# Four-layer graph network on one core: the edge stage's second bias goes through the TensorE accumulator, and VectorE forms a message in one instruction

## The chip, the cores and the metric

The kernel runs on one core of one Trainium2 chip. The metric is the device time of one execution in microseconds (us), lower is better. Where a profile is read, it is one execution on the same core; its time stands beside the median of the timed runs, so that the two are not mixed.

## The reference, cut to what matters

Four graph layers follow each other on 3125 nodes and 103125 edges, sorted by their destination. The change touches only the third, in which every edge builds a message from its source node and its own 64 attributes, and the messages are summed at the destination:

```
ei   = concat(x[src], edge_attr)                  # one row of 256 + 64 per edge
core = maximum(ei @ W1 + b1, 0.0) @ W2 + b2        # b2: the second layer's bias
gate = sigmoid(ei @ Wg + bg)
msg  = gate * core
agg  = segment_sum(msg, dst)
out  = agg + x, then a layer norm with gamma and beta
```

All of it is float32. `b2` is one row of 256 numbers, the same for each edge.

## The kernel before, in words

Each layer is one or more stages, and a stage ends with all engines meeting. The stage of the change is `edge_mlp_pass` (L1539). The node part of `ei @ [W1, Wg]` with its biases has been computed for each node ahead of it and lies in DRAM as `p_table`, 512 numbers a row. The pass then walks over the edges in 102 supertiles of 1024, each of 8 tiles of 128 edges. A loop over 51 pairs of supertiles is unrolled by two, and within a supertile the work is written out in four steps, `k` = 0 to 3, of two tiles each, `y` = 0 and 1. The order on each engine is as written; nothing is rescheduled.

In a step the engines do this for the tile `y`, and PE, DVE and ACT are two tiles (one step) apart from stage to stage:

- PE multiplies the transposed edge attributes (64 rows) by the weights into `psP` (L1756): tile 0 from partitions 0 to 63, tile 1 from partitions 64 to 127.
- DVE adds the gathered node row and writes `pre` (L1659). `pre` holds 256 numbers for the hidden layer and 256 for the gate.
- ACT takes the sigmoid of the second half into `gate` (L1713).
- PE transposes the first half into `psR` (L1770), ACT applies the relu while it copies that into `rT` (L1718), and PE multiplies it by `W2` into `psC` (L1762): two products per tile, each a float32 product of 128 rows by 256 columns.
- DVE adds `b2`, which lies in SBUF copied to all 128 partitions, to `psC` and writes `whole` (L1667), then multiplies `whole` by `gate` in place (L1669). `Link` (L59) makes the second wait for the first.
- ACT rounds two tiles of `whole` to float32r, the high part of `msg` (L1722); POOL subtracts to get the low part (L1595).

Once in a supertile, in step 0, PE transposes the next supertile's attributes (`psEA`, L1731) and DVE builds the one-hot matrix `hot` of the supertile before (L1674 and the helper L763). In step 2 PE sums that supertile's messages with `hot` into `psM`, 16 float32r products (L1737). Where a supertile's destinations span more than one block of 128 nodes, which happens 24 times, there is a round after step 3: DVE adds `psM` to the node sums (L1457), shifts the indices (L1684), builds `xhot`, PE sums again.

The waits that matter: PE's `psP` products wait for DVE's `pre` of the step before (L1753), its `W2` products for `rT` and for the message of the tile that last used the same `psC` (L1759, L1760), its sums for POOL's low parts (L1780). SyncE loads weights and the bias once (L1620 to L1623) and edge attributes per supertile.

Of the kernel before, what the change touches and what calls it, by code (L numbers as in the profile page):

```python
# [19 lines left out]
F32 = mybir.dt.float32  # L20
F32R = mybir.dt.float32r
BF16 = mybir.dt.bfloat16
I32 = mybir.dt.int32
ALU = mybir.AluOpType
# [3 lines left out]
P = 128  # L28
D = 256
# [21 lines left out]
START = 16  # L51
# [23 lines left out]
def hold(eng, sem):  # L75

    eng.sem_inc(sem, 1)


def gnn(nc, a, out, n_nodes, n_edges):  # L80
# [638 lines left out]
    held = top.enter_context(nc.semaphore("held"))  # L719
# [75 lines left out]
    def typed_pass():  # L795

        HALF = SLOTS // 2
        G = H0 * RELS
# [3 lines left out]
        with Stage(("idx_staged", "hotrow", "expanded", "x_hotrow", "x_expanded", "expand_read", "rows_read", "scored",  # L802
# [19 lines left out]
            pick = st.sb("pick", [T_LANES, WT])  # L822
            att = st.sb("att", [P, UT, 2, HALF, H0])
            et = st.sb("et", [P, HALF, 2, UT, G])
# [714 lines left out]
    def edge_mlp_pass():  # L1539
# [1 line left out]


        with Stage(("onehot", "x_onehot", "pre_ps", "pre", "gate", "rT_ps", "rT", "core", "msg", "summed", "added", "x_summed",
                    "x_added", "idx_staged", "high", "split", "link_dve", "link_act", "zeroed", "eaT_ps", "eaT"), ("w_in", "ea0", "ea1")) as st:
            S = st.sem
            DEEP = 4
            LATE = 2
            G_DEEP = SLOTS
            HALF = SLOTS // 2
            table_tile = st.sb("table_tile", [P, 1])  # L1550
            rows = st.sb("rows", [P, 2 * SLOTS, 2 * D])
            stage_idx = st.sb("stage_idx", [P, 2, SLOTS], I32)
# [4 lines left out]
            eaT = st.sb("eaT", [P, 2, HALF, P])  # L1557
            wb = st.sb("wb", [P, 2 * D])
            w2 = st.sb("w2", [P, 2, D])
            b2 = st.sb("b2", [P, D])  # L1560
            pre = st.sb("pre", [P, DEEP, 2 * D])
            gate = st.sb("gate", [P, G_DEEP, D])
            rT = st.sb("rT", [P, DEEP, 2, P])
            whole = st.sb("whole", [P, DEEP, D])
# [4 lines left out]
            psC = [st.ps(f"psC{n}", [P, 512]) for n in range(2)]  # L1569
# [5 lines left out]
            with nc.Block() as block:  # L1575
# [41 lines left out]
                @block.sync  # L1617
                def _(sp):
                    for lo in (0, DE):
                        sp.dma_start(wb[lo:lo + DE, 0:D], a["l2_w1"][D:D + DE, :]).then_inc(S["w_in"], 16)  # L1620
                        sp.dma_start(wb[lo:lo + DE, D:2 * D], a["l2_wg"][D:D + DE, :]).then_inc(S["w_in"], 16)
                    sp.dma_start(w2[:, :, :], a["l2_w2"].rearrange("(c p) d -> p c d", p=P)).then_inc(S["w_in"], 16)
                    sp.dma_start(b2[:, :], a["l2_b2"].partition_broadcast(P)).then_inc(S["w_in"], 16)  # L1623
                    view = a["ea"].rearrange("(s p j) d -> p s (j d)", p=P, j=SLOTS)
                    sp.dma_start(ea[:, 0, :], view[:, 0, :]).then_inc(S["ea0"], 16)
                    with sp.Fori(0, PAIRS) as i:
                        for u in range(2):
                            s = 2 * i + u
                            sp.wait_ge(S["eaT_ps"], START + s)
                            sp.dma_start(ea[:, 1 - u, :], view[:, ds(s + 1, 1), :].squeeze(1)).then_inc(S[f"ea{1 - u}"], 16)  # L1630
                    sp.wait_ge(S["ea0"], 16 * PAIRS + 16)

                @block.vector
                def _(dve):
                    v = nc.vector
                    link = Link(dve, S["link_dve"])

                    v.memset(msg[:, :, :, :, :].bitcast(F32), 0.0)
                    v.memset(hot[:, :, :].bitcast(F32), 0.0)
                    for tile in (table_tile, pre, gate, rT, whole, NODE, psC[0], psC[1]):  # L1640
                        last = v.memset(tile[:, :, :, :] if len(tile.shape) == 4 else
                                        tile[:, :, :] if len(tile.shape) == 3 else tile[:, :], 0.0)
                    last.then_inc(S["zeroed"], 1)
                    dve.wait_ge(S["zeroed"], START + 1)
                    dve.wait_ge(S["w_in"], 96)
                    with dve.Fori(0, PAIRS) as i:
                        for u in range(2):
                            s = 2 * i + u
                            x0, x1, b0, more = work_of(dve, s)
                            link.turn()  # L1650
                            for k in range(HALF):
                                t = SLOTS * s + 2 * k
                                for y in range(2):
                                    j = 2 * k + y
                                    rows_in(dve, i, u, [j])
                                    dve.wait_ge(S["pre_ps"], START + t + y + 1)
                                    dve.wait_ge(S["rT_ps"], START + t + y - DEEP + LATE + 1)
                                    dve.wait_ge(S["gate"], START + t + y - DEEP + 1)
                                    v.tensor_tensor(pre[:, j % DEEP, :], psP[y][:, :], rows[:, u * SLOTS + j, :],  # L1659
                                                    ALU.add).then_inc(S["pre"], 1)  # L1660
                                if k == LATE:
                                    dve.wait_ge(S["summed"], START + s)
                                for y in range(2):
                                    q = (2 * k + y - 2 * LATE) % SLOTS
                                    dve.wait_ge(S["core"], START + t + y + 1)
                                    dve.wait_ge(S["split"], START + HALF * s + k - 1)
                                    link(v.tensor_tensor(whole[:, q % DEEP, :], psC[y][:, 0:D], b2[:, :], ALU.add))  # L1667
                                    dve.wait_ge(S["gate"], START + t + y - 2 * LATE + 1)
                                    v.tensor_tensor(whole[:, q % DEEP, :], whole[:, q % DEEP, :], gate[:, q % G_DEEP, :],  # L1669
                                                    ALU.mult).then_inc(S["msg"], 1)  # L1670
                                if k == 0:
                                    dve.wait_ge(S["summed"], START + s)
                                    hold(dve, held)
                                    link(v.tensor_copy(rel[:, :], dst_of(s - 1)))  # L1674
                                    one_hot(hot[:, :, :], rel[:, :]).then_inc(S["onehot"], 1)
                                if k == HALF - 1:
                                    dve.wait_ge(S["summed"], START + s + 1)
                                    add_block(b0, psM[:, 0:D]).then_inc(S["added"], 1)
                                    dve.wait_ge(S["added"], START + s + 1)
                                    hold(dve, held)  # L1680
                                    with dve.If(more):
                                        with dve.Fori(x0, x1) as x:
                                            link.turn()
                                            link(v.tensor_scalar(rel[:, :], rel[:, :], -float(P), None, ALU.add))  # L1684
                                            one_hot(xhot[:, :, :], rel[:, :]).then_inc(S["x_onehot"], 1)
                                            dve.wait_ge(S["x_summed"], START + x + 1)
                                            add_block(b0 + 1 + x - x0, psM[:, 0:D]).then_inc(S["x_added"], 1)
                                            dve.wait_ge(S["x_added"], START + x + 1)
                                    link.turn()
# [38 lines left out]
                def _(pe):  # L1728
# [9 lines left out]
                                                        start=(j == 0 and n == 0), stop=(j == SLOTS - 1 and n == 1))  # L1738
                        return last

                    pe.wait_ge(S["w_in"], 96)
                    pe.wait_ge(S["zeroed"], START + 1)
                    pe.wait_ge(S["ea0"], 16)
                    transpose_ea(0)
                    with pe.Fori(0, PAIRS) as i:
                        for u in range(2):
                            s = 2 * i + u
                            x0, x1, _, more = work_of(pe, s)
                            for k in range(HALF):
# [4 lines left out]
                                for y in range(2):  # L1754
                                    lo = y * DE
                                    nc.tensor.matmul(psP[y][:, :], eaT[lo:lo + DE, u, k, :], wb[lo:lo + DE, :], start=True,  # L1756
                                                     stop=True).then_inc(S["pre_ps"], 1)
                                for y in range(2):
                                    pe.wait_ge(S["rT"], START + t + y - 1)  # L1759
                                    pe.wait_ge(S["msg"], START + t + y - 1)  # L1760
                                    for c in range(2):
                                        last = nc.tensor.matmul(psC[y][:, 0:D], rT[:, (2 * k + y) % DEEP, c, :], w2[:, c, :],  # L1762
                                                                start=(c == 0), stop=(c == 1))
                                    last.then_inc(S["core"], 1)

                                for y in range(2):
# [978 lines left out]
```

## Time and profile before

| what | value |
|---|---|
| median of 3 runs | 10081.02 us (10074.35 to 10107.51) |
| the profiled execution, its own time | 10087.5 us |
| its span, first to last instruction | 10085.6 us |
| mean granted TensorE clock in it | 0.763 |
| loop of the changed stage | 4026 to 5988 us of the span |

The page gives busy time for each engine. A row of a group gives place, engine, operation and tiles, the shape, the count, the busy time and the mean of one, and behind the last bar how long the engine had been idle before such instructions and who ended that. PE is the matrix product, PEld the load of its stationary operand; one float32 product shows as two records of each (two passes), a float32r product as one. In a row of the timeline the first number is the start, the second the length of the whole run of records.

### The profile page before, as it was taken

The page shows a single profiled execution, that of the slowest core. Times are in us where ns is not written, and L with a number is a line of the kernel's source. Part 1 is how long each engine was busy: PE and PEld are TensorE (multiplying, and loading weights), DVE is VectorE, ACT ScalarE, POOL GpSimd, SP SyncE. Part 2 cuts the span into 40 slices and gives each one's busy share as a digit, 9 for nine tenths or more (in the row PEclk, how much of TensorE's full clock was granted, in tenths as well). Part 3 has the DMA queues.
Part 4 walks back from the last instruction along what each step waited for, and adds up shares of the span by engine and source line. Part 5 has one row for each costly group of instructions (what it writes and reads, how often), then busy time and mean ns, then how long its engine had stood idle before and what let it go on. Part 6 is the DMA issues. An engine that isn't in the chain of part 4 may idle for free. (4 is left out here: it accounts for less than half of the span.)

```text
span 10085.6 us, 117611 instructions
## 1 busy us (share of the span) xinstructions
PE 6095.2 (60%) x25212; PEld 4519.3 (45%) x25213; DVE 5155.4 (51%) x9537; ACT 2745.0 (27%) x6077; POOL 4589.4 (46%) x4782
## 2 busy tenths in 40 slices
PE   4867777753444455989898863454554445455544
PEld 2445656541333343666666642343443333343433
DVE  3258888733222223777777764444344544344444
ACT  0134444421000002444444442222122122222221
POOL 0046555501665640767777742444443233444432
PEclk9978888875776766999999985666666666666666
DMA  3367777711222321444444422332332232332322
GB/s 114 115 193 222 223 217 219 201 47 34 84 85 83 88 69 46 127 119 123 123 122 122 124 82 80 93 93 86 95 93 84 62 92 87 91 92 85 96 83 70
DMA packets 440369, 1100.23 MB, mean 109 GB/s; under 512 B 102512, under 2 KB 177365, under 8 KB 439479
## 3 DMA queue, kind: packets, MB, share of 16 engines
q0 software_dynamic: 249344, 763.23, 26.8%
q1 hardware_dynamic: 190636, 333.56, 10.1%
q14 instruction: 358, 2.93, 0.1%
q8 instruction: 31, 0.51, 0.0%
HBM read 1014.51 MB, written 81.94 MB: 109 GB/s over the span
## 5 line engine op out<-in xcount | busy, mean ns | idle before, releaser
L779 POOL DMA_INDIRECT st_rows<-g_table,st_stage_idx x1632 | 1550.8, 950 | 2019.3 <-DVE st_msg L2385 1541.6
L2564 PE MATMUL st_psM<-st_msg,st_hot 128*128 128x273 f32 x3264 | 1004.1, 470 | 402.6 <-DVE node_values L2338 182.3
L886 POOL DMA_INDIRECT st_rows<-kv_table,st_stage_idx x832 | 825.4, 992 | 590.9 <-PE st_psM L1254 275.5
L2564 PEld LDWEIGHTS st_psM<-st_msg,st_hot 128*128 128x128 f32 x3264 | 747.8, 233 | 629.1 <-issue 413.1
L1586 POOL DMA_INDIRECT st_rows<-p_table,st_stage_idx x816 | 801.6, 982 | 261.4 <-issue 163.5
L779 POOL DMA_INDIRECT st_rows<-h_table,st_stage_idx x816 | 777.9, 953 | 263.2 <-issue 260.8
L1762 PE MATMUL st_psC<-st_w,st_rT 128*128 128x256 f32 x3264 | 815.4, 393 | 0.5 <-DVE st_whole L1669 0.5
L1762 PEld LDWEIGHTS st_psC<-st_w,st_rT 128*128 128x128 f32 x3264 | 587.8, 190 | 381.9 <-ACT st_rT L1718 203.8
L1659 DVE TENSOR_TENSOR st_pre<-st_psP,st_rows 128x512 f32<-128x512 f32 x816 | 524.5, 685 | 409.5 <-PE st_psP L1756 280.2
L1595 POOL TENSOR_TENSOR st_msg<-st_whole,st_msg 128x512 fp32r<-128x512 f32 x408 | 565.0, 1385 | 350.4 <-ACT st_msg L1722 343.3
L2477 ACT ACTIVATE st_low<-st_dm 128x8 f32<-128x8 f32 x252 | 51.9, 206 | 2459.4 <-DVE st_dm L2328 1982.6
L1522 PE MATMUL st_psM<-st_rows,st_hot 128*128 128x256 f32 x1632 | 443.2, 434 | 365.5 <-issue 123.6
L1228 PE MATMUL st_psE<-st_q_rows,st_hotrow 104*128 104x256 f32 x1664 | 548.6, 502 | 42.2 <-issue 33.6
L2396 DVE TENSOR_TENSOR_SCAN st_psX<-st_pens,st_psX 24x1024 f32<-24x1024 bf16 x68 | 155.2, 2283 | 790.8 <-DMA h_table<-st_h 388.2
L1522 PEld LDWEIGHTS st_psM<-st_rows,st_hot 128*128 128x128 f32 x1632 | 358.0, 222 | 448.0 <-issue 325.1
L1713 ACT ACTIVATE st_gate<-st_pre 128x256 f32<-128x256 f32 x816 | 330.0, 416 | 761.7 <-DVE st_pre L1659 742.3
L1756 PE MATMUL st_psP<-st_wb,st_eaT 64*128 64x512 f32 x1632 | 472.2, 656 | 56.4 <-DVE st_pre L1659 50.2
L1228 PEld LDWEIGHTS st_psE<-st_q_rows,st_hotrow 104*128 104x128 f32 x1664 | 424.0, 261 | 145.4 <-issue 53.1
L2594 PE MATMUL st_psW<-ident,st_seg 24*128 24x24 f32 x544 | 61.7, 257 | 701.5 <-DVE st_seg L2397 701.5
L2385 DVE TENSOR_TENSOR st_msg<-st_rows,st_psU 128x2048 f32<-128x2048 f32 x204 | 464.8, 2279 | 2.0 <-ACT st_psU L2503 2.0
L2564 PE MATMUL st_psZ<-st_msg,st_xhot 128*128 128x273 f32 x768 | 309.6, 558 | 217.5 <-issue 137.2
L1254 PE MATMUL st_psM<-st_rows,st_hot 128*128 128x262 f32 x1632 | 397.7, 398 | 66.7 <-issue 56.0
(406 smaller groups left out, 11630.1 us busy)
## 6 DMA issues: line engine op xcount, KB each, us to landing
st_dst_row<-in_dst_row SPq DMA_DIRECT2D x310, 512.0 KB
kv_table<-st_rows_out SPq DMA_DIRECT2D x25, 1560.0 KB, 5.6
st_ea<-in_ea SPq DMA_DIRECT2D x103, 256.0 KB
st_rows<-g_table,st_stage_idx POOLq DMA_INDIRECT x1632
st_pens<-pen_table SPq DMA_DIRECT2D x208, 72.0 KB
st_rows<-kv_table,st_stage_idx POOLq DMA_INDIRECT x832
st_rows<-h_table,st_stage_idx POOLq DMA_INDIRECT x816
st_rows<-p_table,st_stage_idx POOLq DMA_INDIRECT x816, 3.5
```

What stands on the lines that cost most here:

```text
L779: pool.indirect_dma_start(out=rows[:, slot, j, :], out_offset=None, in_=table, in_offset=bass.IndirectOffsetOnAxis(ap=stage_idx[:, g, u * ...
L886: pool.indirect_dma_start(out=rows[:, slot, j, :], out_offset=None, in_=kv_table, in_offset=bass.IndirectOffsetOnAxis(ap=stage_idx[:, g, u ...
L1228: last = nc.tensor.matmul(psE[h][:, j * D:(j + 1) * D], onehots[0:NQ, h * HALF + j, :], queries, start=(fresh and j % 2 == 0), stop=True, ...
L1254: last = nc.tensor.matmul(out[:, 0:SUM_W], onehots[:, j, :], rows[:, slot, j, D:D + SUM_W], start=(j == 0), stop=(j == SLOTS - 1))
L1522: last = nc.tensor.matmul(out[:, 0:D], onehots[:, j, :], rows[:, slot, j, :], start=(j == 0), stop=(j == SLOTS - 1))
L1586: pool.indirect_dma_start(out=rows[:, u * SLOTS + j, :], out_offset=None, in_=p_table, in_offset=bass.IndirectOffsetOnAxis(ap=stage_idx[:, ...
L1595: nc.gpsimd.tensor_tensor(msg[:, half, q:q + 2, 1, :], whole[:, q % DEEP:q % DEEP + 2, :], msg[:, half, q:q + 2, 0, :].bitcast(F32), ALU.s ...
L1659: v.tensor_tensor(pre[:, j % DEEP, :], psP[y][:, :], rows[:, u * SLOTS + j, :], ALU.add).then_inc(S["pre"], 1)
L1756: nc.tensor.matmul(psP[y][:, :], eaT[lo:lo + DE, u, k, :], wb[lo:lo + DE, :], start=True, stop=True).then_inc(S["pre_ps"], 1)
L1762: last = nc.tensor.matmul(psC[y][:, 0:D], rT[:, (2 * k + y) % DEEP, c, :], w2[:, c, :], start=(c == 0), stop=(c == 1))
L2385: v.tensor_tensor(msg[:, u, :, 0:GAT_W].rearrange("p j (h c) -> p j h c", h=H3)[:, :, :, 0:HW3 - 1], rows[:, slot, :, 0:D].rearrange("p j ...
L2564: last = nc.tensor.matmul(out[:, 0:MSG_W], onehots[:, j, :], msg[:, u, j, :], start=(j == 0), stop=(j == SLOTS - 1))
```

## The change

The bias is no longer added by DVE. SyncE loads it twice, into partitions 0 and 32 of a tile `b2_in` of 33 rows that DVE has cleared. DVE makes `b2` from it in float32r: row 0 is the rounded value (the high half), row 32 the remainder (the low half), the rest are zeros. For each tile of edges PE first multiplies a block of ones (33 by 128) by `b2` (33 by 256) into `psC`, as the start of the accumulation, and the two `W2` products add to it. DVE then reads `psC` and `gate` and writes the finished message to `whole` in one instruction.

```
-            b2 = st.sb("b2", [P, D])
+            b2_in = st.sb("b2_in", [B_ROWS, D])          # B_ROWS = LOW + 1 = 33
+            b2 = st.sb("b2", [B_ROWS, D], F32R)
+            ones_b = st.sb("ones_b", [B_ROWS, P], F32R)
...
-                    sp.dma_start(b2[:, :], a["l2_b2"].partition_broadcast(P)).then_inc(S["w_in"], 16)
+                    sp.wait_ge(S["cleared"], START + 1)
+                    for row in (0, LOW):
+                        sp.dma_start(b2_in[row:row + 1, :], a["l2_b2"].unsqueeze(0)).then_inc(S["w_in"], 16)
...
+                    v.memset(ones_b[:, :].bitcast(F32), 1.0)
+                    v.memset(b2_in[:, :], 0.0).then_inc(S["cleared"], 1)
...
+                    link(v.tensor_copy(b2[:, :], b2_in[:, :]))
+                    v.tensor_tensor(b2[LOW:B_ROWS, :], b2_in[LOW:B_ROWS, :], b2[LOW:B_ROWS, :].bitcast(F32),
+                                    ALU.subtract).then_inc(S["bias"], 1)
...
-                                    link(v.tensor_tensor(whole[:, q % DEEP, :], psC[y][:, 0:D], b2[:, :], ALU.add))
+                                    hold(dve, held)
                                     dve.wait_ge(S["gate"], START + t + y - 2 * LATE + 1)
-                                    v.tensor_tensor(whole[:, q % DEEP, :], whole[:, q % DEEP, :], gate[:, q % G_DEEP, :],
+                                    v.tensor_tensor(whole[:, q % DEEP, :], psC[y][:, 0:D], gate[:, q % G_DEEP, :],
                                                     ALU.mult).then_inc(S["msg"], 1)
...
+                    pe.wait_ge(S["bias"], START + 1)
...
                                     pe.wait_ge(S["rT"], START + t + y - 1)
                                     pe.wait_ge(S["msg"], START + t + y - 1)
+                                    nc.tensor.matmul(psC[y][:, 0:D], ones_b[:, :], b2[:, :], start=True, stop=False)
                                     for c in range(2):
                                         last = nc.tensor.matmul(psC[y][:, 0:D], rT[:, (2 * k + y) % DEEP, c, :], w2[:, c, :],
-                                                                start=(c == 0), stop=(c == 1))
+                                                                start=False, stop=(c == 1))
```

On PE the change shows in each step of the loop. This is step 0 of a supertile before, from the top of the loop's body; `psC` are the `W2` products, `psP` and `psEA` those of the attributes.

```order
L1756 MATMUL st_psP<-st_wb,st_eaT 128x512 x2
L1759 REGISTER_ALU
L1762 MATMUL st_psC<-st_w,st_rT 128x256 x4
L1770 MATMUL st_psR<-ident,st_pre 128x128 x4
L1774 ISA
L1731 MATMUL st_psEA<-ident,st_ea 128x128 x4
```

And the same place now, where the line numbers have moved by 12 or 13:

```order
L1768 MATMUL st_psP<-st_wb,st_eaT 128x512 x2
L1771 REGISTER_ALU
L1773 MATMUL st_psC<-st_b,st_ones_b 128x256
L1775 MATMUL st_psC<-st_w,st_rT 128x256 x2
L1773 MATMUL st_psC<-st_b,st_ones_b 128x256
L1775 MATMUL st_psC<-st_w,st_rT 128x256 x2
L1783 MATMUL st_psR<-ident,st_pre 128x128 x4
L1787 ISA
L1742 MATMUL st_psEA<-ident,st_ea 128x128 x4
```

One short product stands behind `psP` and another between the two tiles' `W2` products; nothing else has moved on PE.

On DVE, in step 0 between `pre` and the next step's `pre`, this stands before; `rel` and `hot` are the indices and the one-hot matrix:

```order
L1659 TENSOR_TENSOR st_pre<-st_psP,st_rows 128x512
L1666 REGISTER_ALU
L1667 TENSOR_TENSOR st_whole<-st_psC,st_b 128x256
L1669 TENSOR_TENSOR st_whole<-st_whole,st_gate 128x256
L1667 TENSOR_TENSOR st_whole<-st_psC,st_b 128x256
L1669 TENSOR_TENSOR st_whole<-st_whole,st_gate 128x256
L1672 REGISTER_ALU
L1674 ISA
L1674 COPY st_rel<-dst_rel 128x8
L763 TENSOR_TENSOR st_hot<-st_rel,iota_row 128x1024
```

And now:

```order
L1670 TENSOR_TENSOR st_pre<-st_psP,st_rows 128x512
L1677 REGISTER_ALU
L1680 TENSOR_TENSOR st_whole<-st_psC,st_gate 128x256 x2
L1683 REGISTER_ALU
L1685 ISA
L1685 COPY st_rel<-dst_rel 128x8
L763 TENSOR_TENSOR st_hot<-st_rel,iota_row 128x1024
```

Four instructions on `whole` have become two; their place among the others is the same.

## Rows read from the trace of the kernel before

**Rows 1.** The page: busy time of the engines, and the granted TensorE clock by slices.
```profile
PE 6095.2 (60%) x25212; PEld 4519.3 (45%) x25213; DVE 5155.4 (51%) x9537; ACT 2745.0 (27%) x6077; POOL 4589.4 (46%) x4782
...
PEclk9978888875776766999999985666666666666666
```

**Rows 2.** The loop's stretch: length, busy PE, PEld, DVE, ACT, POOL, clock, DMA.
```profile
4026.00:5988.00 1962.00, 1764.19 (x8950) 1239.97 (x8948) 1416.28 (x2826) 942.50 (x2241) 1369.16 (x1313) 0.97 0.42 121
```

**Rows 3.** Groups of that stretch: count, busy us, mean ns, idle us before.
```profile
L1762 PE MATMUL st_psC<-st_w,st_rT 128*128 128x256 f32 x3264 | 815.4, 393 | 0.5 <-DVE st_whole L1669 0.5
...
L1595 POOL TENSOR_TENSOR st_msg<-st_whole,st_msg 128x512 fp32r<-128x512 f32 x407 | 563.8, 1385 | 346.4 <-ACT st_msg L1722 339.3 <-issue 2.3
...
L1669 DVE TENSOR_TENSOR st_whole<-st_whole,st_gate 128x256 f32<-128x256 f32 x816 | 391.4, 480 | 27.9
L1667 DVE TENSOR_TENSOR st_whole<-st_psC,st_b 128x256 f32<-128x256 f32 x816 | 339.0, 415 | 1.2 <-PE st_psC L1762 1.2
...
L1722 ACT CAST st_msg<-st_whole 128x512 fp32r<-128x512 f32 x407 | 252.1, 619 | 206.4 <-DVE st_whole L1669 171.9 <-issue 23.7
...
L1737 PEld LDWEIGHTS st_psM<-st_msg,st_hot 128*128 128x128 f32 x1632 | 201.0, 190 | 66.7 <-issue 66.6
...
L1737 PE MATMUL st_psM<-st_msg,st_xhot 128*128 128x256 f32 x384 | 83.3, 400 | 97.4 <-DVE st_xhot L763 97.4
...
L1731 PEld LDWEIGHTS st_psEA<-ident,st_ea 128*128 128x128 f32 x408 | 47.7, 142 | 0.0
```

**Rows 4.** Waits of that stretch: us in total, times, longest.
```profile
PEld st_psP L1756 <- DVE st_pre L1659: 86.9, 135, 1.1
```

**Rows 5.** Timeline of PE over one supertile: start, length of the run.
```profile
5008.87 0.60 PE L1770 MATMUL st_psR<-ident,st_pre 128*128 128x128 f32 x4
5009.30 0.60 PE L1731 MATMUL st_psEA<-ident,st_ea 128*128 128x128 f32 x4
5009.83 1.13 PE L1756 MATMUL st_psP<-st_wb,st_eaT 64*128 64x512 f32 x4
5010.89 1.99 PE L1762 MATMUL st_psC<-st_w,st_rT 128*128 128x256 f32 x8
5012.72 0.60 PE L1770 MATMUL st_psR<-ident,st_pre 128*128 128x128 f32 x4
5013.47 1.13 PE L1756 MATMUL st_psP<-st_wb,st_eaT 64*128 64x512 f32 x4
...
5017.35 2.17 PE L1737 MATMUL st_psM<-st_msg,st_hot 128*128 128x256 f32 x16 [0.40 <-POOL st_msg L1595]
5019.46 1.13 PE L1756 MATMUL st_psP<-st_wb,st_eaT 64*128 64x512 f32 x4
```

**Rows 6.** Timeline of PEld where the attribute product waits for nobody.
```profile
5022.87 0.30 PEld L1756 LDWEIGHTS st_psP<-st_wb,st_eaT 64*128 64x128 f32 x4 [0.17 <-issue]
```

**Rows 7.** PE in an early stage: a 35-row float32r product between 128-row ones.
```profile
380.73 2.54 PE L661 MATMUL st_psY<-st_w,st_hT 128*128 128x256 f32 x11
383.20 0.38 PE L664 MATMUL st_psY<-st_b,st_hot 35*128 35x256 f32 x1
383.51 0.44 PE L651 MATMUL st_psT<-ident,st_h 128*128 128x128 f32 x2
```

**Rows 8.** DVE ahead of one extra round.
```profile
4998.17 0.42 DVE L1667 TENSOR_TENSOR st_whole<-st_psC,st_b 128x256 f32<-128x256 f32 x1
...
4998.62 0.43 DVE L1669 TENSOR_TENSOR st_whole<-st_whole,st_gate 128x256 f32<-128x256 f32 x1
```

**Rows 9.** Stretches of 16 sums with `xhot` and of 16 with `hot`; clock third from the end.
```profile
5002.56:5006.04 3.48, 3.48 (x18) 3.35 (x18) 0.00 (x0) 0.00 (x0) 1.68 (x2) 0.57 0.41 101
5017.35:5019.52 2.17, 2.17 (x18) 2.04 (x18) 0.82 (x3) 0.70 (x2) 1.85 (x3) 1.00 0.42 106
```

More of the change, by code:

```diff
@@ L1543, in edge_mlp_pass @@
         with Stage(("onehot", "x_onehot", "pre_ps", "pre", "gate", "rT_ps", "rT", "core", "msg", "summed", "added", "x_summed",
-                    "x_added", "idx_staged", "high", "split", "link_dve", "link_act", "zeroed", "eaT_ps", "eaT"), ("w_in", "ea0", "ea1")) as st:
+                    "x_added", "idx_staged", "high", "split", "link_dve", "link_act", "zeroed", "cleared", "bias", "eaT_ps", "eaT"), ("w_in", "ea0", "ea1")) as st:
             S = st.sem
@@ L1549, in edge_mlp_pass @@
             HALF = SLOTS // 2
+            LOW = 32
+            B_ROWS = LOW + 1
             table_tile = st.sb("table_tile", [P, 1])
@@ L1644, in _ @@
                     dve.wait_ge(S["zeroed"], START + 1)
-                    dve.wait_ge(S["w_in"], 96)
+                    dve.wait_ge(S["w_in"], 112)
+                    link(v.tensor_copy(b2[:, :], b2_in[:, :]))
+                    v.tensor_tensor(b2[LOW:B_ROWS, :], b2_in[LOW:B_ROWS, :], b2[LOW:B_ROWS, :].bitcast(F32),
+                                    ALU.subtract).then_inc(S["bias"], 1)
                     with dve.Fori(0, PAIRS) as i:
@@ L1739, in sum_up @@
                         return last
-                    pe.wait_ge(S["w_in"], 96)
+                    pe.wait_ge(S["w_in"], 112)
                     pe.wait_ge(S["zeroed"], START + 1)
+                    pe.wait_ge(S["bias"], START + 1)
                     pe.wait_ge(S["ea0"], 16)
```

## The prediction

> **What bounds the kernel now.** I read the page first. No engine is busy for more than 60% of the span [rows 1], so the total says little, and the question belongs to the one stage that the change touches. Its loop runs from 4026 to 5988 us; the clock slices stand at 9 there. The stretch by itself [rows 2]: PE busy for 1764 of 1962 us (90%), DVE 1416 (72%), POOL 1369 (70%), ACT 943 (48%), clock 0.97. So PE is the first suspect, and the change adds work to PE and takes it from DVE.
>
> A PE that is 90% busy could still be kept waiting by its partners, so I next took the timeline of PE over one supertile, to see what follows on what [rows 5]. Four 128-column passes of `psR` start at 5008.87 and the next run, `psEA`, at 5009.30: 0.43 us, 0.107 a pass, with no gap. From that a 256-column float32 pass is 0.215, and eight of `psC` are 1.72; `psR` follows `psC` after 1.83 (5010.89 to 5012.72), so 0.11 is extra, the first operand load that nothing covers. Four `psP` passes of 64 rows and 512 columns take 1.06, not 4 x 0.43 = 1.72: the two tiles run side by side in the two halves of the array, two rounds of 0.43, plus 0.11 for the load and 0.10. From `psEA` to `psP` it is 0.53: 0.43 and again 0.10. The 16 sums take 2.11 (5017.35 to 5019.46): 16 x 0.119, and the same 0.11 and 0.10. The pattern: a run follows another of the same height at once; between a 128-row run and a 64-row run there are 0.10 us of nothing and 0.11 of uncovered load.
>
> So the chain through the loop is PE's own, apart from three waits:
> - `psP` for DVE's `pre`: PEld stands idle for 86.9 us in 135 places [rows 4]; 0.17 of each is there without a wait too [rows 6], which leaves 86.9 - 135 x 0.17 = 64 us. In rows 5 it is 0.75 instead of 0.53 at 5012.72.
> - the sums for POOL's low part: PEld idle for 66.7 us over 102 supertiles, where the `psEA` loads, which also follow `psR`, have 0.0 [rows 3]. 67 us.
> - the 24 extra rounds: PE idle for 97.4 us, 4.06 each [rows 3].
>
> **The change, part by part.**
>
> *The bias products on PE: 816, two in each of 408 steps.* The trace has a product of nearly this form, 35 rows, float32r, 256 columns, between 128-row runs [rows 7]. Eleven passes of 0.215 that start at 380.73 end at 383.10; the 35-row product starts at 383.20, the next run at 383.51, and that one pays its own uncovered load. So one such product between 128-row runs costs 0.10 + 0.31 + 0.11 = 0.52 us, of which 0.11 is streaming. The bias product of tile 1 stands between the `W2` products of tile 0 and tile 1, all of 128 rows: this case. 408 x 0.52 = 212 us.
>
> The bias product of tile 0 comes behind `psP`, which is of 64 rows, and ahead of `W2`. The change of height behind `psP` is paid already. If 33 rows go by the half-array, as the 64 of `psP`, its load is covered by `psP`'s last round and it costs one pass: 0.12 by the sums' pace. If each run of short products ends for itself, it costs 0.31. No row shows a 33-row behind a 64-row product. I take 0.12, the nearer to how rows 5 read (same height, no gap): 408 x 0.12 = 49 us; the other end, 126 us, is kept for the range. Below 0.12 I see nothing, since no other work is at hand to stream beside it.
>
> The Trainium skill, TensorEngine Tiling (Array Packing), Key Properties, says that changing the tiling mode, though not merely the tile, drains TensorE. It gives no time for it; the 0.10 us of nothing in rows 5 and 7 fit it.
>
> Together 261 us on PE.
>
> *One instruction fewer on DVE per message.* What goes is the multiplication in SBUF, 391.4 us in all; the one that stays reads PSUM as L1667 does, 0.415 [rows 3]. DVE would be busy for some 1025 of the loop's time. DVE is not the chain, so this pays only in the three waits:
> - `pre`: where PE waits for it, in step 1, DVE had the two messages and the one-hot matrix ahead of it. Now DVE has 2 x 0.48 less to do and PE takes 0.64 longer per step. The mean wait was 64/135 = 0.5, less than either, so it goes whole: -64.
> - the low part of step 1: behind it are ACT's 0.62 and POOL's 1.39 [rows 3]. The wait is 0.65 a supertile. The message comes 0.45 earlier behind its product, and PE has a longer step 2 in front of the sum, 0.64: 1.1 against 0.65. It goes whole: -67. POOL's two gathers and one subtraction, in all 1369 us of the stretch, don't bind.
> - the extra rounds: PE waits for a chain that begins with the last `W2` product and runs over both DVE instructions. Their starts are 0.45 apart [rows 8], and that falls out: -24 x 0.45 = -11. The rest of the 4.06 stays.
>
> Together -142. All of it is what DVE's relief can give, since PE waits for nobody else.
>
> *What else is touched.* Two small transfers in place of one, behind a memset that DVE does first; the zeroing that follows covers them. The conversion and the subtraction on 33 partitions stand between the zeroing and PE's start: not in the trace, 0 to 2 us once by rows such as L1667's; I take 1. The `held` increment on DVE takes the place of the `Link` wait, nothing. POOL's subtraction, slowed at times, sees less DVE traffic in SBUF; it is off the chain.
>
> **Sum.** +212 + 49 - 142 + 1 = +120 us on the profiled execution's 10087.5: 10207.5. That execution is 6.5 above the median of the runs, so 10201; I say 10200 us, +1.2%.
>
> **The rivals.**
>
> A, faster: the bias product streams in line, like a 17th sum, for 0.12 us wherever it stands. Then PE pays 816 x 0.12 = 98, gets back 142, and the time is 10081 + 98 - 142 + 1 = 10038. For it: the sums are float32r and take that [rows 5]. Against: these have 128 rows, and the row with 35 costs four times that [rows 7]. It decides at 0.17 us a product (141/816). The Trainium skill, TensorE: Matmul & The Clock Gate, Why this matters for your kernels, says that a single product of 32 rows takes the same time as one of 128. By that rule this rival would hold; here it would cover the 0.11 us of streaming, and the 0.41 around it in rows 7 speak against reading it for the whole cost. 6%.
>
> B: the product behind `psP` is separated too: 212 + 126 - 142 + 1 = +197, 10278. For it: no row excludes it. 12%.
>
> C: the waits don't go, because they move: DVE hands the message over earlier, yet `pre` or the low part is late for another reason (gathered rows, POOL's gathers). Then +262 at most, 10343; with half of them 10272. For it: POOL is 70% busy. Against: it idles 346 us ahead of its subtractions [rows 3], so it has room. 7%.
>
> D: most of it is hidden: PE is held by `rT` and the bias product fills that wait. Against: the 1.06 between `psP` and `psC` in rows 5 is used up by streaming, load and 0.10. It would end within 30 us of now. 3%.
>
> My forecast has the other 72%. One gain beside it: the sums of an extra round run at a granted clock of 0.57 after the 4 us wait, 3.48 us against 2.17 at 1.00 [rows 9]. If a wait shorter by 0.45 kept the clock at its upper level (2.4 GHz), 24 x 1.3 = 31 us would come back; I expect none of it, and keep it for the lower end.
>
> **How the numbers follow.** Lower end: the clock's 31 and some 15 for an operand load partly covered, 10150. Upper end: rival B, 10278, or half of C, 10272, so 10285. That leaves out A, D and the worse half of C, some 15%. Less than 0.3%, 30 us, can't be told from no change here. Faster: A without its dearer end, 5%. Same: the rest of A and D, 4%. Slower: 91%.
>
> **What would show it.** In the changed profile `psR` starts about 2.47 us behind the first record of `psC` (1.83 now), of which some 0.52 lie around the second bias product, with idle PEld on both sides; PE's waits on `pre` and on POOL's low part are near zero; the extra rounds wait for about 3.6 us; DVE in the loop is near 1025 us busy; the loop takes near 2080 us, and the other stages are as before. I am wrong if the second bias product starts 0.215 behind the pass ahead of it and the next 0.12 behind it (A), or if PE's idle time has stayed with another releaser (C).

## Result, and the profile after

The changed kernel takes 10213.48 us (median of 4 runs, 10196.74 to 10224.62), the one before 10078.16 (4 runs, 10074.35 to 10107.51). The ratio is 1.0125, 95% interval 1.0108 to 1.0142: slower. Forecast were 10200 us and 10150 to 10285.

The stretch of the loop in the changed kernel's profile, with the columns of [rows 2]:

```profile
4058.00:6120.00 2062.00, 1974.21 (x9766) 1346.37 (x9763) 1094.95 (x2010) 933.50 (x2242) 1390.90 (x1313) 0.98 0.41 115
```

The loop is 2062 us long and was 1962. DVE is busy for 321 us less and PE for 96% of the loop instead of 90%: PE sets the pace of the loop and now hardly stops. The groups of that stretch, which answer to [rows 3]:

```profile
L1599 POOL TENSOR_TENSOR st_msg<-st_whole,st_msg 128x512 fp32r<-128x512 f32 x407 | 522.8, 1284 | 425.4 <-ACT st_msg L1733 421.0
L1773 PE MATMUL st_psC<-st_b,st_ones_b 33*128 33x256 f32 x816 | 436.7, 535 | 0.0
L1680 DVE TENSOR_TENSOR st_whole<-st_psC,st_gate 128x256 f32<-128x256 f32 x816 | 341.7, 423 | 329.0 <-PE st_psC L1775 268.8 <-issue 23.8 <-ACT st_gate L1724 15.2
...
L1748 PEld LDWEIGHTS st_psM<-st_msg,st_hot 128*128 128x128 f32 x1632 | 201.2, 190 | 0.2
...
L1748 PE MATMUL st_psM<-st_msg,st_xhot 128*128 128x256 f32 x384 | 74.7, 370 | 87.3 <-DVE st_xhot L763 87.3
```

The idle time ahead of the ordinary sums has gone from 66.7 to 0.2 us, that ahead of the extra sums from 97.4 to 87.3, and DVE now waits 269 us for PE where it waited 1. The 0.535 us of a bias product is a modelled duration; what it costs is read from the starts. The timeline of PE in one step and the beginning of the next, which answers to [rows 5]:

```profile
5012.78 1.13 PE L1768 MATMUL st_psP<-st_wb,st_eaT 64*128 64x512 f32 x4
5013.34 0.68 PE L1773 MATMUL st_psC<-st_b,st_ones_b 33*128 33x256 f32 x1
5013.95 1.13 PE L1775 MATMUL st_psC<-st_w,st_rT 128*128 128x256 f32 x4
5015.01 0.38 PE L1773 MATMUL st_psC<-st_b,st_ones_b 33*128 33x256 f32 x1
5015.32 1.13 PE L1775 MATMUL st_psC<-st_w,st_rT 128*128 128x256 f32 x4
5016.29 0.60 PE L1783 MATMUL st_psR<-ident,st_pre 128*128 128x128 f32 x4
5016.82 1.13 PE L1768 MATMUL st_psP<-st_wb,st_eaT 64*128 64x512 f32 x4
```

From `psP` to the first `W2` product it is 1.17 us, where it was 1.06: the first bias product costs 0.11. From that to `psR` it is 2.34 instead of 1.83: the second costs 0.51. And `psR` to `psP` in step 1 is 0.53, the value without a wait, where it was 0.75.

### The profile page after: what moved, and what is told of

Read it like the earlier page. It is cut to its first block and busy times, and to the rows that moved or that the text cites. A ratio compares the mean times of both kernels' runs of the same rounds, so it can differ in the third digit from the quotient of the medians.

```text
span 10222.8 us, 118029 instructions
## 1 busy us (share of the span) xinstructions
PE 6321.1 (62%) x26028; PEld 4634.6 (45%) x26029; DVE 4835.5 (47%) x8725; ACT 2734.6 (27%) x6077; POOL 4605.5 (45%) x4782
## 5 line engine op out<-in xcount | busy, mean ns | idle before, releaser
L2577 PEld LDWEIGHTS st_psM<-st_msg,st_hot 128*128 128x128 f32 x3264 | 752.2, 235 | 609.9 <-issue 391.4
L1590 POOL DMA_INDIRECT st_rows<-p_table,st_stage_idx x816 | 841.4, 1031 | 261.1 <-issue 172.9
L1775 PE MATMUL st_psC<-st_w,st_rT 128*128 128x256 f32 x3264 | 923.8, 405 | 0.0
L1599 POOL TENSOR_TENSOR st_msg<-st_whole,st_msg 128x512 fp32r<-128x512 f32 x408 | 524.0, 1284 | 430.1 <-ACT st_msg L1733 425.7
L1775 PEld LDWEIGHTS st_psC<-st_w,st_rT 128*128 128x128 f32 x3264 | 553.5, 189 | 280.0 <-issue 185.6
L1680 DVE TENSOR_TENSOR st_whole<-st_psC,st_gate 128x256 f32<-128x256 f32 x816 | 341.7, 423 | 329.0 <-PE st_psC L1775 268.8
```

What stands on the lines that cost most here:

```text
L1590: pool.indirect_dma_start(out=rows[:, u * SLOTS + j, :], out_offset=None, in_=p_table, in_offset=bass.IndirectOffsetOnAxis(ap=stage_idx[:, ...
L1599: nc.gpsimd.tensor_tensor(msg[:, half, q:q + 2, 1, :], whole[:, q % DEEP:q % DEEP + 2, :], msg[:, half, q:q + 2, 0, :].bitcast(F32), ALU.s ...
L2577: last = nc.tensor.matmul(out[:, 0:MSG_W], onehots[:, j, :], msg[:, u, j, :], start=(j == 0), stop=(j == SLOTS - 1))
```

## The experiments

The chips differ. Each ratio below is against the kernel before, run beside it on the same chip, and the loop is read from each profile. On the chips of all experiments but the last the kernel before takes 8232 to 8238 us, on that of the last 10004.

**Both kernels again, on another chip.**

> The kernel before, unchanged, profiled on the chip that runs the others of this call: its loop should take 1960 us as in the first profile, whatever its gather stages take, since PE sets it. Theory 1: differences between the first two profiles outside the loop (some 35 us) are of the executions, not of the change.

> The changed kernel, unchanged, on the same chip as the others of this call. Theory 1: loop near 2062 us, 101 us over the one before, and the time over that of the kernel before by the same 100 us (95 to 110), so a ratio near 1.012 on a chip where the kernel takes 8235 us. Rival: the change costs another 30 us outside its stage, 130 to 135 us in all.

Measured: 8234.6 us for the one before, and 8340.77 against 8237.61 for the changed one, ratio 1.0125 (1.011 to 1.0141). Where the first and the last `W2` product start: the four line views are of before and changed on the first chip, then of before and changed on this one:

```profile
L1762 PE MATMUL st_psC<-st_w,st_rT x3264: 379/379/793, 4026.1 to 5986.7; 128*128 128x256 f32 x192
```
```profile
L1775 PE MATMUL st_psC<-st_w,st_rT x3264: 379/379/793, 4058.2 to 6118.7; 128*128 128x256 f32 x192
```
```profile
L1762 PE MATMUL st_psC<-st_w,st_rT x3264: 379/379/793, 3547.2 to 5507.4; 128*128 128x256 f32 x192
```
```profile
L1775 PE MATMUL st_psC<-st_w,st_rT x3264: 379/379/794, 3554.4 to 5615.2; 128*128 128x256 f32 x192
```

The loop takes 1960.6, 2060.5, 1960.2 and 2060.8 us: it is the same on both chips, and grows by 100 on each. The kernel grows by 103 on this chip and by 135 on the first. There the loop also begins 32 us later, here 7 later. Of the 7, the new preparation of the bias accounts for some 2: from DVE's last instruction of the stage before to the first `W2` product it is 34.7 us in the kernel before and 36.6 in the changed one. The rest of the delay builds up in earlier stages, whose code is the same. So the loop is worth 100 us, and some 30 us of the first comparison came from elsewhere. Theory 1's "of the executions" isn't shown: the lowest of the four changed runs there lies 89 above the highest of before, and no repeat on that chip separates the execution from its data's place in memory.

**The bias product at full height.** `B_ROWS` is what sets the height; the low half is still formed in row 32 alone:

```
-            B_ROWS = LOW + 1
+            B_ROWS = P
```

> The bias product of the changed kernel, made 128 rows high: ones and b2 have 128 partitions, the bias's high half in row 0, the low half in row 32, zeros in the others. Theory 1 (the cost is the change of height between 33-row and 128-row runs): each bias product costs one pass of 0.12 us, 98 us in all; PE's waits stay gone (about 150 us of the kernel before), so the loop takes 1905 to 1920 us (before 1962, changed 2062) and the kernel is 0.4 to 0.6% faster than before, near 10035 us. PsR starts 1.95 to 2.1 us behind the first W2 pass. Theory 2 (the cost is the change of type, float32 to float32r and back, whatever the height): 0.3 to 0.5 us around each bias product as now, loop near 2060, 1.2% slower than before.

Measured: 8216.77 against 8235.37, ratio 0.9978 (0.9968 to 0.9988), loop 1938 us. One step on PE:

```profile
4528.29 1.13 PE L1768 MATMUL st_psP<-st_wb,st_eaT 64*128 64x512 f32 x4
4529.35 0.38 PE L1773 MATMUL st_psC<-st_b,st_ones_b 128*128 128x256 f32 x1
4529.57 1.03 PE L1775 MATMUL st_psC<-st_w,st_rT 128*128 128x256 f32 x4
4530.24 0.47 PE L1773 MATMUL st_psC<-st_b,st_ones_b 128*128 128x256 f32 x1
4530.55 1.03 PE L1775 MATMUL st_psC<-st_w,st_rT 128*128 128x256 f32 x4
4531.41 0.60 PE L1783 MATMUL st_psR<-ident,st_pre 128*128 128x128 f32 x4
```

From `psP` to `psR` it is now 3.12 us, against 3.51 with the short products and 2.89 with none: 0.23 for both products instead of 0.62. The starts inside that stretch are uneven (0.22, 0.67, 0.31 and 0.86 us apart), so only the sum is read, and 0.12 each is a mean. Same type, same columns, four times the rows, and 0.39 us less. The height it is, not the type. The loop is 18 us over the upper end of what I expected. Against the changed kernel it should have lost 408 x 0.39 = 159 us and lost 124. Of the 35 that are missing, PE's wait ahead of the ordinary sums takes 24 (23.9 us, where it was 0.2), and the 384 extra sums, which take 84.3 instead of 74.7, take 10. What makes PE wait is the next question.

**Both short products behind the other short runs.** The waits are split so that both bias products come ahead of both pairs of `W2` products:

```
 for y in range(2):
-    pe.wait_ge(S["rT"], START + t + y - 1)
     pe.wait_ge(S["msg"], START + t + y - 1)
     nc.tensor.matmul(psC[y][:, 0:D], ones_b[:, :], b2[:, :], start=True, stop=False)
+for y in range(2):
+    pe.wait_ge(S["rT"], START + t + y - 1)
```

> The bias products stay 33 rows high but both stand directly behind the two 64-row attribute products, ahead of the four W2 products; the second no longer stands between 128-row runs. Theory 1 (height): 0.12 us each, loop 1905 to 1920 us, 0.4 to 0.6% faster than before. Theory 2 (type): one group with a gap on both sides, about 0.43 a step, loop near 1985, 0.2% slower than before. If taking psC two products earlier makes PE wait for the message of the step before, a wait of PE on DVE's whole shows behind the attribute products; by the present trace the message is there some 0.5 us ahead, so I expect none.

Measured: 8214.63 against 8235.37, ratio 0.9977 (0.9968 to 0.9986), loop 1938 us. The loop is as long as at full height, with the same 23.9 us of wait ahead of the sums.

```profile
4523.62 1.13 PE L1768 MATMUL st_psP<-st_wb,st_eaT 64*128 64x512 f32 x4
4524.19 0.80 PE L1772 MATMUL st_psC<-st_b,st_ones_b 33*128 33x256 f32 x2
4524.91 1.99 PE L1776 MATMUL st_psC<-st_w,st_rT 128*128 128x256 f32 x8
4526.74 0.60 PE L1784 MATMUL st_psR<-ident,st_pre 128*128 128x128 f32 x4
```

`psP` to `psR` is 3.12 again. Nothing but the order has changed against the changed kernel, and 0.39 us a step have gone. Two 33-row products behind 64-row ones cost 0.11 to 0.12 each; what is dear is to go down and up once more.

**No bias product.** The first `W2` product of each tile starts the accumulation again, as in the kernel before:

```
-                                    nc.tensor.matmul(psC[y][:, 0:D], ones_b[:, :], b2[:, :], start=True, stop=False)
```

> No bias product at all: the second layer's bias is left out of the messages; DVE keeps the one instruction per message. What DVE's relief alone gives. Theory 1: it alone removes PE's waits on pre (64 us), on the low part (67) and 0.45 of each of 24 extra rounds (11): loop near 1815 us, kernel near 9935 us, 1.4% faster than before. Rival (the waits went because PE's steps grew longer, not because DVE has less to do): half of these waits remain, loop 1850 to 1900, 0.6 to 1.1% faster.

Measured: 8179.38 against 8235.37, ratio 0.9931 (0.9918 to 0.9945), loop 1898: 64 us less than before, not 147. That lies in the range of the rival. The idle time ahead of the sums and the attribute products, and POOL over one supertile:

```profile
L1748 PEld LDWEIGHTS st_psM<-st_msg,st_hot 128*128 128x128 f32 x1632 | 201.0, 190 | 75.4 <-issue 75.4
L1768 PEld LDWEIGHTS st_psP<-st_wb,st_eaT 64*128 64x128 f32 x1628 | 126.4, 190 | 65.8 <-issue 48.7 <-DVE st_pre L1670 3.2
```
```profile
4527.92 1.28 POOL L1599 TENSOR_TENSOR st_msg<-st_whole,st_msg 128x512 fp32r<-128x512 f32 x1
4529.36 0.97 POOL L1590 DMA_INDIRECT st_rows<-p_table,st_stage_idx  x1 [0.16 <-issue]
4530.63 0.94 POOL L1590 DMA_INDIRECT st_rows<-p_table,st_stage_idx  x1 [0.30 <-issue]
4531.59 1.28 POOL L1599 TENSOR_TENSOR st_msg<-st_whole,st_msg 128x512 fp32r<-128x512 f32 x1
```

The wait on `pre` is gone (3.2 us of 86.9), as forecast. That on the low part is not: 75.4 us. POOL goes from subtraction to subtraction in 3.67 us without waiting for any engine (the 0.16 and 0.30 us in the rows have no releaser), and PE's step without a bias product is 3.42. The sums that follow the last subtraction shown start 0.33 us behind its end, after an idle PE of 1.03 us that the trace puts down to it. POOL is what is late there, though it is busy for 72% of the stretch.

**DVE's two instructions kept.** The first of them adds a tile of zeros:

```
-                                    hold(dve, held)
+                                    link(v.tensor_tensor(whole[:, q % DEEP, :], psC[y][:, 0:D], none[:, :], ALU.add))
                                     dve.wait_ge(S["gate"], START + t + y - 2 * LATE + 1)
-                                    v.tensor_tensor(whole[:, q % DEEP, :], psC[y][:, 0:D], gate[:, q % G_DEEP, :],
+                                    v.tensor_tensor(whole[:, q % DEEP, :], whole[:, q % DEEP, :], gate[:, q % G_DEEP, :],
```

> The bias products of the changed kernel with DVE's two instructions kept: DVE adds a tile of zeros to psC and then multiplies by the gate. What PE's longer steps do without DVE's relief. Theory 1: a step longer by 0.62 us is longer than the mean waits on pre (0.5) and about as long as that on the low part (0.65), so most of them are gone without any relief of DVE: loop 2070 to 2090 us, kernel 0.1 to 0.3% slower than the changed one. Rival (only DVE's relief removes the waits): loop near 2200, 1.3% slower than the changed one.

Measured: 8349.58 against 8235.37, ratio 1.0142 (1.0127 to 1.0158), loop 2075: 13 us over the changed kernel.

```profile
L1749 PEld LDWEIGHTS st_psM<-st_msg,st_hot 128*128 128x128 f32 x1632 | 201.2, 190 | 0.9 <-issue 0.8
```

With DVE as busy as ever (1427 us), the wait on the low part is gone: PE's step of 4.04 us is longer than POOL's 3.67. In the changed kernel the one-instruction message is worth 13 us, nearly all of it in the extra rounds: here PE waits 96.0 us ahead of the extra sums instead of 87.3, and these take 77.5 instead of 74.7.

**POOL's gathers spread.** In `turn`, the eight gathers of a supertile come 1, 1, 3, 3 over the steps instead of two each, so that the subtraction of step 1, for which the sums wait, has one gather ahead of it:

```
-                                gather(1 - u, 2 * k)
-                                gather(1 - u, 2 * k + 1)
+                                for j in ((0,), (1,), (2, 3, 4), (5, 6, 7))[k]:
+                                    gather(1 - u, j)
```

With the full-height product:

> The full-height bias product of e1, and POOL's gathers spread 1, 1, 3, 3 over the four steps instead of 2 each, so that POOL's subtractions of steps 0 and 1 come earlier. Theory (POOL's step of two gathers and one subtraction, 3.7 us, is longer than PE's 3.66 and sets PE's wait ahead of the sums): that wait goes to its floor, 25 us less, loop near 1913 us, kernel 0.5 to 0.6% faster than before. Rival (the wait is DVE's or ACT's lateness): loop near 1938 as e1, 0.2% faster.

In the kernel before:

> The kernel before with only POOL's gathers spread 1, 1, 3, 3. Theory (POOL sets the wait ahead of the sums): of its 67 us most go, 40 to 65, loop 1895 to 1920 us, 0.5 to 0.8% faster than before, with no bias product and DVE's two instructions kept. Rival (DVE's two instructions set it): under 15 us, within 0.2% of before.

Measured with the full-height product: 8205.9 against 8237.61, ratio 0.9964 (0.995 to 0.9978), loop 1923. The wait ahead of the ordinary sums is 0.0 (23.9 with two each), so POOL it was; but that ahead of the extra sums has grown from 87.3 to 99.7, which takes 12 back, and the kernel gains 0.4% where 0.5 to 0.6 was expected. In the kernel before: 8185.26, ratio 0.9938 (0.9924 to 0.9951), loop 1908, 53 us less. The size was in the expected range and the reason was not: the wait ahead of the ordinary sums has hardly moved (62.3), so in that kernel POOL isn't alone there: the subtraction of step 1 now waits for ACT in nearly every supertile, 1.37 us as a rule. What moved is the extra rounds: PE waits 72.5 us ahead of their sums instead of 97.4, and the sums themselves take 65.5 instead of 83.7. That is 43 of the 53 us. Their groups, in the kernel before and in the one with the spread:

```profile
L1684 DVE TENSOR_SCALAR st_rel<-st_rel 128x8 f32<-128x8 f32 x24 | 29.7, 1240 | 13.2 <-DVE node_values L1457 13.2
```
```profile
L1737 PE MATMUL st_psM<-st_msg,st_xhot 128*128 128x256 f32 x384 | 65.5, 336 | 72.5 <-DVE st_xhot L763 72.5
...
L1684 DVE TENSOR_SCALAR st_rel<-st_rel 128x8 f32<-128x8 f32 x24 | 4.4, 182 | 13.2 <-DVE node_values L1457 13.2
```

Shifting eight numbers a partition took DVE 1.24 us and takes 0.18 now. That accounts for the 25 us of wait. The timeline of the kernel before, ahead of an extra round, shows beside what:

```profile
4999.88 1.26 POOL L1595 TENSOR_TENSOR st_msg<-st_whole,st_msg 128x512 fp32r<-128x512 f32 x1 [1.23 <-ACT st_msg L1722]
4999.93 1.24 DVE L1684 TENSOR_SCALAR st_rel<-st_rel 128x8 f32<-128x8 f32 x1 [0.55 <-DVE node_values L1457]
5001.21 1.22 DVE L763 TENSOR_TENSOR st_xhot<-st_rel,iota_row 128x1024 fp32r<-128x1024 f32 x1
```

The shift begins 0.05 us after POOL's subtraction and ends with it. In the changed kernel it begins 0.12 ahead of the subtraction and takes 0.17, and the one-hot behind it takes the hit:

```profile
5002.06 0.17 DVE L1695 TENSOR_SCALAR st_rel<-st_rel 128x8 f32<-128x8 f32 x1 [0.54 <-DVE node_values L1457]
5002.18 1.26 POOL L1599 TENSOR_TENSOR st_msg<-st_whole,st_msg 128x512 fp32r<-128x512 f32 x1 [2.24 <-ACT st_msg L1733]
5002.27 2.25 DVE L763 TENSOR_TENSOR st_xhot<-st_rel,iota_row 128x1024 fp32r<-128x1024 f32 x1
```

That gives a new theory: a DVE instruction between SBUF tiles stands still while POOL's subtraction runs.

**The test of it.** First with one gather more in step 3 (1, 1, 2, 4), and the spread in the kernel before once more beside it:

> The full-height bias product, and POOL's gathers spread 1, 1, 2, 4, so that the subtraction of step 3 starts some 1.2 us later than with 1, 1, 3, 3. Theory (DVE's one-hot for an extra round stands still for as long as POOL's subtraction in SBUF runs beside it): the 24 one-hots take 1.23 us instead of 2.76, PE's wait ahead of the extra sums falls from 4.75 to near 3.2, the wait ahead of the ordinary sums stays at its floor: loop 1870 to 1890 us, kernel 0.9 to 1.1% faster than before. Rival (the one-hot is long for another reason): loop near 1923 as with 1, 1, 3, 3, 0.4% faster; or the subtraction comes so late that the sums of the next supertile wait again.

> The kernel before with POOL's gathers spread 1, 1, 3, 3, once more, on the same chip as the one above, so that the two can be compared: 0.6% faster than before, loop near 1907 us; by the theory the one above is 0.3 to 0.4% faster still.

Measured: 8201.95 against 8232.33, ratio 0.9958 (0.9944 to 0.9971), loop 1924, one-hots still 2.77 us; and 8183.76, ratio 0.994 (0.9926 to 0.9953). By the letter that went to the rival, but the subtraction had not moved: POOL works through steps 2 and 3 without a stop, and there are six gathers in them either way. So the edit didn't test the theory. Its profile says something all the same. In 22 of the 24 rounds the subtraction starts 0.53 to 0.57 us behind the one-hot, which then takes 2.90 to 2.94. In the other two it starts 0.99 behind, or not at all while the one-hot runs, and the one-hot takes 1.28 and 1.23. A long round and a short one:

```profile
4503.20 2.91 DVE L763 TENSOR_TENSOR st_xhot<-st_rel,iota_row 128x1024 fp32r<-128x1024 f32 x1
4503.75 1.27 POOL L1599 TENSOR_TENSOR st_msg<-st_whole,st_msg 128x512 fp32r<-128x512 f32 x1
4504.95 1.20 POOL L1585 COPY st_stage_idx<-src_idx 128x8 int32 x1
...
4731.87 1.28 DVE L763 TENSOR_TENSOR st_xhot<-st_rel,iota_row 128x1024 fp32r<-128x1024 f32 x1
4732.86 1.43 POOL L1599 TENSOR_TENSOR st_msg<-st_whole,st_msg 128x512 fp32r<-128x512 f32 x1
4734.23 0.19 POOL L1585 COPY st_stage_idx<-src_idx 128x8 int32 x1
```

Standing still while the subtraction runs isn't the whole account either: a long one-hot loses 1.68 us here, and the subtraction takes 1.27.

The experiment was put right in one more (1, 0, 2, 5: seven in these two steps), here against the full-height kernel with 1, 1, 3, 3:

```
-                                for j in ((0,), (1,), (2, 3, 4), (5, 6, 7))[k]:
+                                for j in ((0,), (), (1, 2), (3, 4, 5, 6, 7))[k]:
```

> The full-height bias product, and POOL's gathers spread 1, 0, 2, 5: one more between the subtractions of step 1 and step 3 than with 1, 1, 3, 3 and with 1, 1, 2, 4 (both have six there, which is why the subtraction of step 3 did not move). Theory (DVE's one-hot stands still while POOL's subtraction runs beside it): the subtraction of step 3 now starts after the one-hot has ended, the 24 one-hots take 1.23 us instead of 2.77, PE waits 3.2 instead of 4.75 ahead of the extra sums: loop 1875 to 1890 us, kernel 0.8 to 1.0% faster than before. Rival (something else makes them long): loop near 1923, 0.4% faster. If the late gathers make DVE wait for rows, a wait of pre on the gathers shows and the gain is smaller.

Measured: 9952.79 against 10004.08, ratio 0.995 (0.9932 to 0.9967), loop 1895, on a chip of the slower kind; 51 us less in the kernel, where 0.8 to 1.0% was expected, and 66 less in the loop than the 1961 of the kernel before, whose profile is from another chip. The groups that decide, and one of the rounds:

```profile
L1768 PEld LDWEIGHTS st_psP<-st_wb,st_eaT 64*128 64x128 f32 x1628 | 125.9, 189 | 75.3 <-issue 38.8 <-DVE st_pre L1670 22.3
L1748 PE MATMUL st_psM<-st_msg,st_xhot 128*128 128x256 f32 x384 | 69.5, 351 | 62.7 <-DVE st_xhot L763 57.5 <-issue 5.2
L763 DVE TENSOR_TENSOR st_xhot<-st_rel,iota_row 128x1024 fp32r<-128x1024 f32 x24 | 29.4, 1225 | 0.8
```

All 24 one-hots take 1.23 us, now that no subtraction runs beside them, and PE waits 2.6 us ahead of the extra sums instead of 4.15. The theory holds for what the one-hot costs. The loop stays 5 to 20 us above what was expected: PE waits for `pre` again, 22.3 us in 75 places. It isn't late rows. In each of the 75 places DVE had waited shortly before for POOL's subtraction, now behind five gathers, before it could write the next message; over the loop that wait is 94.3 us, and 37.9 with 1, 1, 3, 3. One of them:

```profile
4202.33 0.76 DVE L1680 TENSOR_TENSOR st_whole<-st_psC,st_gate 128x256 f32<-128x256 f32 x2 [1.36 <-POOL st_msg L1599]
4205.69 0.30 PEld L1768 LDWEIGHTS st_psP<-st_wb,st_eaT 64*128 64x128 f32 x4 [0.31 <-DVE st_pre L1670]
```

The loops side by side, in us: before 1961, changed 2062, full height 1938, full height with the last spread 1895, the kernel before with 1, 1, 3, 3 1908 and 1913. The best two kernels, the old one with its gathers spread and the full-height one with the last spread, are 0.6% and 0.5% faster than before; they ran on different chips, and their intervals overlap.

## Why the prediction was right, and where not

- *What bounds the loop.* Right. PE's own sequence is 96% of the changed loop, its time is the same on chips where the whole kernel differs by 1800 us, and it follows the order and height of PE's products: full height and both short products together give the same 3.12 us from `psP` to `psR` and the same loop of 1938.
- *The second bias product.* 0.52 forecast from [rows 7], 0.51 measured. The full-height and the grouped kernel show that it is the change of height on both sides, and nothing else about the product.
- *The first bias product.* 0.12 taken, 0.11 measured; the other end, 0.31, is excluded, and with it rival B, and D too, since both products show their cost. One sign of "What would show it" was misplaced: the first bias product starts 0.56 us behind `psP`, inside its run, so from the first record of `psC` to `psR` it is 2.95 and not 2.47. From `psP` it is 3.51, against the forecast's 3.53. Together 253 us instead of 261.
- *What comes back.* 142 forecast, 153 found (1962 + 253 - 2062). The sum was right and its reason partly wrong. The step that failed is "All of it is what DVE's relief can give, since PE waits for nobody else". Relief alone gives 64 us (no bias product); PE's longer step alone gives 140 (DVE's two instructions: 1962 + 253 - 2075). For the low part I weighed both, and needed the longer step; but I set POOL aside as not binding on the strength of its 70% and its idle 346 us. Of these, 191 lie in the extra rounds and 117 ahead of the last subtraction of each supertile, for which no sums wait directly. Ahead of the subtractions of steps 1 and 2 POOL waits for no engine in any of 101 supertiles, and its 3.67 us stand against PE's 3.42. So the 67 us would not have come back without the slow product that hid them. The 11 us of surplus are the sums of the extra rounds, below.
- *The extra rounds.* 0.45 each forecast, 0.42 found: the wait fell from 4.06 to 3.64. I took the rest of the 4.06 for fixed; 1.04 of it was DVE standing still, as the kernel before with its gathers spread shows (72.5 us in 24 rounds, 3.02 each).
- *DVE's work.* Forecast near 1025 us in the loop, measured 1095. Its records overlapped more in the kernel before (the groups add up to some 1516 us where it was busy for 1416), so taking the 391.4 off the busy time took off too much. No term of the sum hangs on it.
- *The clock.* The 384 extra sums fell from 83.3 to 74.7 us, so 9 of the 31 us I kept for the lower end came (the round at 5004.66 has a granted clock of 0.68 and takes 2.88 us; rows 9 have 0.57 and 3.48). The shorter wait alone isn't why: at full height PE waits the same 87.3 us and the sums take 84.3. Nor does one kernel always give the same: the kernel before with its gathers spread had 65.5 in one execution and 69.5 in another, with a wait of 72.5 in both. Why the clock fell less in the changed kernel stays open.
- *Rivals.* A is false as a statement on the 33-row product and true of one of 128 rows: 0.12 each, and faster than before, by 0.2% and not by 0.4%, since the low part still waits and the extra sums are slow again. C did not occur in the changed kernel; its mechanism, POOL, shows where PE's step is shorter: 23.9 us of wait with the full-height or the grouped products, 75.4 with none, and 0.0 once the gathers are spread.
- *The total.* Forecast +120, of which the loop has 100: the two sizes that were off, 8 us on the products and 11 on what comes back, go the same way. The preparation, put at 1, took 2. On the second chip the whole is +103. The 135 of the first comparison hold 32 that no term of mine has; that 10213 lies so near 10200 is in part luck. The cause of those 32 is open.

## What to carry to other kernels

Count a product on TensorE by what stands on both sides of it: a short one among tall ones costs 0.5 us here for 0.11 of streaming, and making it full height with zero rows, or moving it beside other short ones, takes 0.4 of that away. Before an engine's relief is booked as gain, look for the next one whose own cycle lies near that of the engine that sets the pace (here POOL's 3.67 us against PE's 3.42 without the bias products, 3.65 with full-height ones and 4.04 with short ones): a busy share over the whole loop doesn't show it, its gaps over the few steps ahead of the wait do. And try the small thing first: the order of POOL's gathers alone, with no arithmetic touched, gave more (0.6%) than the whole exchange between DVE and PE at full height (0.2%).

## What the runs showed of the hardware that was not expected

In these profiles a DVE instruction from SBUF to SBUF waits for POOL's subtraction in SBUF to end: 128x8 numbers in 1.24 us beside it and 0.17 without, 128x1024 in 2.25 or 2.91 and 1.23. The gathers beside the one-hot in the last experiment didn't hold it. A head start of 0.55 us brings the one-hot nothing: it ends 1.09 us behind the subtraction's end, and 1.08 behind where it starts 0.09 after the subtraction. A head start of 0.99 was enough: 1.28 us, and that subtraction took 1.43 instead of 1.27. Why is open. POOL waits too: its copy of 128x8 indices takes 1.18 to 1.21 us when it comes beside the held one-hot, ending with it, and 0.19 otherwise.

In the kernel before, DVE's instruction that reads PSUM (L1667) keeps to 0.409 to 0.425 us over all 816, while its neighbour that has both inputs in SBUF (L1669) averages 0.480 and takes up to 1.33. The change replaces these two by one that reads PSUM. Where an instruction is late, look at what POOL does in that very microsecond.

The kernel before takes 8235 us on three chips and 10004 to 10081 on two, with this loop at 1960 on both kinds.
